# Turning the softmax maxima: on TensorE with a copy by ScalarE, or in 32 by 32 squares on VectorE with four DMAs

## The reference

```python
def _L0_xattn_ref(q, k, v, wq_w, wq_b, wk_w, wk_b, wv_w, wv_b, wo_w, wo_b):
    wq = (q @ wq_w.T + wq_b).reshape(b, t, H, DH)
    wk = (k @ wk_w.T + wk_b).reshape(b, t, H, DH)
    wv = (v @ wv_w.T + wv_b).reshape(b, t, H, DH)
    scores = jnp.einsum('bthd,bshd->bhts', wq, wk) / jnp.sqrt(jnp.float32(DH))
    probs = jax.nn.softmax(scores, axis=-1)
    attn = jnp.einsum('bhts,bshd->bthd', probs, wv)
    return attn.reshape(b, t, d) @ wo_w.T + wo_b

x = x + _L0_xattn_ref(_layernorm(x), ctx_1024, ctx_1024, ...)
x = x + _L0_ffn_ref(_layernorm(x), Wg, ln_scale, ln_bias, W1, b1, W2, b2)   # 8 experts, the best one by its logit
```

## Time and profile before

| | |
|---|---|
| median of 3 runs | 1424.43 us (1423.45 to 1425.28) |
| the profiled execution | 1425.39 us, of which the span from the first to the last instruction is 1423.6 us |
| mean granted TensorE clock | 0.992 |
| busy, share of the span | TensorE 97%, its weight loads 84%, VectorE 81%, ScalarE 69%, GpSimd 34% |
| 48 to 975 us (attention): busy | TensorE 907.6, VectorE 788.7, ScalarE 676.4, GpSimd 276.0 of 927 us |
| DMA | 168870 packets, 207.46 MB, 146 GB/s in the mean |

### The profile page before, as it was taken

The page is one execution under the profiler, slowest core; times in us unless marked ns, Lnnn a source line. Parts: engine busy times, 40 slices in busy tenths (PEclk is TensorE's granted clock), DMA queues, the critical chain, the costliest instruction groups (busy, mean ns, idle before and its releaser), DMA issues.

```text
span 1423.6 us, 40094 instructions
## 1 busy us (share of the span) xinstructions
PE 1380.6 (97%) x15314; PEld 1196.9 (84%) x15314; DVE 1158.0 (81%) x2760; ACT 985.6 (69%) x1664; POOL 482.8 (34%) x662
## 2 busy tenths in 40 slices
PE   6899999999999999999999999988999999999998
PEld 5688888888888888888888888876888888888887
DVE  4688888888888888888888888876787878878776
ACT  5477777777777777777777777756667666676764
POOL 4222332233322332233223332324444444444430
PEclk8899999999999999999999999999999999999999
DMA  6656665567656665667566755643343434434322
GB/s 183 144 146 184 171 185 150 159 172 178 161 150 175 174 176 151 167 174 182 154 159 168 185 152 154 167 114 105 91 126 106 127 105 120 117 108 132 102 80 75
DMA packets 168870, 207.46 MB, mean 146 GB/s; under 512 B 19895, under 2 KB 119530, under 8 KB 168682
## 3 DMA queue, kind: packets, MB, share of 16 engines
q1 hardware_dynamic: 168682, 204.89, 54.2%
HBM read 69.26 MB, written 33.81 MB: 72 GB/s over the span
## 4 chain that ended last, share of the span: by engine, by line
PE 88%; DVE 6%; ACT 2%; issue 2%; DMA 1%; POOL 0%; SPq 0%; ACTq 0%; DVEq 0%; POOLq 0%
PE s_ps L1345 13%; PE pp_ps L1219 11%; PE st_ps L1153 8%; PE pv_ps L1167 8%; PE s_ps L1125 8%; PE pp_ps L1192 7%; PE pp_ps L1227 6%; PE st_ps L1370 6%; PE pp_ps L1370 6%; PE pv_ps L1175 4%; PE pp_ps L1213 3%; DVE negmax L830 2%; PE pp_ps L1309 2%; PE t_ps L1144 2%; PE t_ps L1320 1%
## 5 line engine op out<-in xcount | busy, mean ns | idle before, releaser
L644 ACT ACTIVATE pT<-st_ps 128x1024 f32<-128x1024 f32 x256 | 263.1, 1028 | 108.0 <-PE st_ps L1153 107.1
L830 DVE TENSOR_REDUCE negmax<-s_ps 128x8 f32<-128x1024 f32 x256 | 311.2, 1215 | 24.3 <-PE s_ps L1125 24.0
L501 POOL TENSOR_TENSOR q_parts<-q,q_parts 128x1024 bf16<-128x1024 f32 x32 | 68.5, 2141 | 403.3 <-ACT q_parts L638 403.3
L700 ACT ACTIVATE pT<-s_ps,c 128x512 f32<-128x512 f32 x128 | 87.8, 688 | 119.4 <-PE s_ps L1345 114.3
L1125 PE MATMUL s_ps<-k_packed,q_packed 96*128 96x128 bf16 x2048 | 158.0, 220 | 11.2 <-DVE negmax L830 5.8
L1345 PE MATMUL s_ps<-k_packed,w_hi 128*128 128x512 f32 x512 | 165.8, 415 | 0.0
L1153 PE MATMUL st_ps<-q_packed,k_packed 98*128 98x128 bf16 x2048 | 158.1, 220 | 1.5 <-DMA q_packed<-negmaxT 1.5
L1125 PEld LDWEIGHTS s_ps<-k_packed,q_packed 96*128 96x128 bf16 x2048 | 128.1, 98 | 29.7 <-DVE negmax L830 17.5
L1153 PEld LDWEIGHTS st_ps<-q_packed,k_packed 98*128 98x128 bf16 x2048 | 120.6, 98 | 27.3 <-issue 25.0
L513 POOL TENSOR_TENSOR xb<-xin,bo_all 128x256 f32<-128x256 f32 x128 | 90.4, 728 | 150.8 <-DMA x_scratch<-xb 133.1
L1167 PE MATMUL pv_ps<-pT,v 128*32 128x128 f32 x4096 | 138.7, 276 | 0.0
(11 more groups left out here) (199 smaller groups left out, 3679.1 us busy)
## 6 DMA issues: line engine op xcount, KB each, us to landing
q_packed<-q_parts SPq DMA_DIRECT2D x192, 256.0 KB, 4.3
k_packed<-k_parts SPq DMA_DIRECT2D x192, 256.0 KB, 4.6
xin<-in_x_dram SPq DMA_DIRECT2D x32, 512.0 KB, 3.9
cin<-in_ctx_dram SPq DMA_DIRECT2D x32, 512.0 KB, 4.6
out_dram<-xb SPq DMA_DIRECT2D x32, 512.0 KB, 3.2
x_scratch<-xb SPq DMA_DIRECT2D x32, 256.0 KB, 4.8
x_scratch<-xb SPq DMA_DIRECT2D x64, 128.0 KB, 4.7
k_parts<-mask_scratch SPq DMA_DIRECT2D x32, 256.0 KB, 4.0
```

The source lines that it names most:

```text
L644: a.activation(pT[u % 2][:], st_ps[:], ACT.Exp, scale=DH ** -0.5).then_inc(s_exp, 1)
L700: a.activation(hidden32[m], h_ps[m % 2], ACT.Gelu, bias=c1[:, m:m + 1]).then_inc(f_he, 1)
L830: v.tensor_reduce(own, s_ps[:].rearrange("p (h s) -> p h s", s=P), AX_X, ALU.max, negate=True).then_inc(s_red, 1)
```

## The change

VectorE has an instruction that turns each square of 32 by 32 elements in place of the whole tile. `negmax_wide` becomes `negmax_hl`, 128 x 32, and after the low half of the second unit of a batch VectorE turns it into `negmaxT`, now 128 x 32: the strip of partitions 32q to 32q + 31 holds the 32 kinds (half, head) for the 32 queries 32q to 32q + 31. Four DMAs take the four strips to `q_packed`, each 32 rows of 64 bytes. They add 64 to the semaphore for a batch. `turn_max`, `keep_max`, the cleared columns and their semaphores are gone; `turn_attn` no longer waits for the copy of the maxima.

```diff
-        negmax_wide = [sb(f"negmax_wide{n}", [P, P], BF16) for n in range(2)]
-        negmaxT = [sb(f"negmaxT{n}", [2 * H, P], BF16) for n in range(2)]
+        negmax_hl = [sb(f"negmax_hl{n}", [P, 2 * H], BF16) for n in range(2)]
+        negmaxT = [sb(f"negmaxT{n}", [P, 2 * H], BF16) for n in range(2)]
...
             def load_max(n, b):
-                sp.wait_ge(s_mte, at(PAIRS, n, b + 1))
-                sp.dma_start(packed[0][n % 2][KP:KP + 2, :, b * T:(b + 1) * T], negmaxT[b % 2][:]).then_inc(ld_mx[b % 2], 16)
+                sp.wait_ge(s_mt, at(PAIRS, n, b + 1))
+                for q in range(P // (2 * H)):
+                    strip = slice(q * 2 * H, (q + 1) * 2 * H)
+                    sp.dma_start(packed[0][n % 2][KP:KP + 2, :, b * T + q * 2 * H:b * T + (q + 1) * 2 * H],
+                                 negmaxT[b % 2][strip, :]).then_inc(ld_mx[b % 2], 16)
...
-            def keep_max(n, b):
-
-                act.wait_ge(s_mt, at(PAIRS, n, b + 1))
-                wait(act, ld_mx[b % 2], 16 * at(PAIRS // 2, n, b // 2))
-                a.copy(negmaxT[b % 2][:], maxT_ps).then_inc(s_mte, 1)
...
                 v.tensor_tensor(lo, own, hi, ALU.subtract).then_inc(s_mp, 1)
+                if m == C - 1:
+                    dve.wait_ge(s_mp, at(UNITS, n, u + 1))
+                    wait(dve, ld_mx[b % 2], 64 * at(PAIRS // 2, n, b // 2))
+                    v.transpose(negmaxT[b % 2][:], negmax_hl[b % 2][:]).then_inc(s_mt, 1)
...
-            def turn_max(n, b):
-                pe.wait_ge(s_mp, at(UNITS, n, C * (b + 1)))
-
-                wait(pe, s_mte, at(PAIRS, n, b))
-                done = turned_at(n, C * b - 2) if b > 0 else turned_at(n - 1, UNITS - 2)
-                if done:
-                    pe.wait_ge(s_ate, at(GB, *done) + 1)
-                t.transpose(maxT_wide, negmax_wide[b % 2][:], ident_bf[:]).then_inc(s_mt, 1)
...
             def scoresT(n, u):
...
-                pe.wait_ge(ld_mx[b % 2], 16 * (at(PAIRS // 2, n, b // 2) + 1))
+                pe.wait_ge(ld_mx[b % 2], 64 * (at(PAIRS // 2, n, b // 2) + 1))
```

More of the change, by code:

```diff
@@ L128, in xattn_moe @@
         w1_raw = pT[1][:].rearrange("p (c e h) -> p c e h", c=C, e=E)
-        negmax_p = [wide[:, 0:2 * H].rearrange("p (i j m) -> p i j m", i=2, m=C) for wide in negmax_wide]
+        negmax_p = [hl[:].rearrange("p (i j m) -> p i j m", i=2, m=C) for hl in negmax_hl]
         recip = sb("recip", [P, H])
@@ L193, in xattn_moe @@
             "ffn_bias_in_psum", "ffn_bias_kept", "bo_in_psum", "ffn_weights_step"))
-        s_rowh, s_wide = sem("bias_rows_by_head"), sem("max_columns_cleared")
+        s_rowh = sem("bias_rows_by_head")
         ld_x, ld_c = [sem(f"x_loaded{n}") for n in range(2)], sem("ctx_loaded")
@@ L207, in xattn_moe @@
         s_r, s_mid, s_lo = sem("remainder_done"), sem("mid_done"), sem("lo_done")
-        s_s, s_red, s_hi, s_mp, s_mt, s_mte, s_st, s_exp, s_pv, s_rc, s_nrm = (sem(n) for n in (
-            "scores_ready", "max_done", "max_hi_done", "max_parts_done", "max_transposed", "max_kept",
+        s_s, s_red, s_hi, s_mp, s_mt, s_st, s_exp, s_pv, s_rc, s_nrm = (sem(n) for n in (
+            "scores_ready", "max_done", "max_hi_done", "max_parts_done", "max_transposed",
             "scoresT_ready", "exp_done", "pv_ready", "recip_done", "attn_normed"))
@@ L483, in _ @@
             g.memset(far_sel[:], 0.0).then_inc(s_pc, 1)
-            for wide in negmax_wide:
-                g.memset(wide[:, 2 * H:P], 0.0).then_inc(s_wide, 1)
             def norm(n):
@@ L678, in _ @@
                 item(1, k)
-            keep_max(0, 0)
             def keep_xT(n, c):
@@ L721, in group @@
                 for u in range(UNITS):
-                    nxt = later(n, u, 2)
                     done = turned_at(n, u)
@@ L741, in group @@
                             item(n + ahead, k)
-                    if nxt and u % 2 == 0:
-                        keep_max(nxt[0], nxt[1] // 2)
                     if more2 and u == 2:
@@ L1127, in scores, with turn_attn @@
                 mm.then_inc(s_s, 1)
-            def turn_max(n, b):
-                pe.wait_ge(s_mp, at(UNITS, n, C * (b + 1)))
-                wait(pe, s_mte, at(PAIRS, n, b))
-                done = turned_at(n, C * b - 2) if b > 0 else turned_at(n - 1, UNITS - 2)
-                if done:
-                    pe.wait_ge(s_ate, at(GB, *done) + 1)
-                t.transpose(maxT_wide, negmax_wide[b % 2][:], ident_bf[:]).then_inc(s_mt, 1)
-            def turn_attn(n, b, kept):
+            def turn_attn(n, b):
                 pe.wait_ge(s_nrm, at(GB, n, b + 1))
-                if kept:
-                    pe.wait_ge(s_mte, at(PAIRS, kept[0], kept[1] // 2 + 1))
+                if n == 0 and b == 0:
+                    pe.wait_ge(s_bo, 1)
+                wait(pe, s_ate, at(GB, n, b))
                 for c in range(C):
@@ L1292, in _ @@
             item(1, 5)
-            pe.wait_ge(s_wide, 2)
-            turn_max(0, 0)
             scores(0, 2)
@@ L1375, in even @@
             def even(n, u):
-                ahead, nxt, done, kept = later(n, u, 3), later(n, u, 2), turned_at(n, u), turned_at(n, u + 1)
+                ahead, done, kept = later(n, u, 3), turned_at(n, u), turned_at(n, u + 1)
                 if ahead:
@@ L1395, in odd @@
             def odd(n, u):
-                ahead, nxt, done = later(n, u, 3), later(n, u, 1), turned_at(n, u)
+                ahead, done = later(n, u, 3), turned_at(n, u)
                 if ahead:
@@ L1406, in odd @@
                 if done:
-                    turn_attn(*done, nxt)
+                    turn_attn(*done)
                 if n == LAST and u == 7:
@@ L1423, in _ @@
             hidden(0, 1)
-            turn_attn(LAST, GB - 1, None)
+            turn_attn(LAST, GB - 1)
             mask(0)
```

4 lines of the change are left out of this document (removed).

## The result

The changed kernel is slower: 1468.76 us in the median (1466.94 to 1470.10) against 1423.94 us before, a ratio of 1.0317 (95% interval 1.0303 to 1.0331). That is 44.8 us more. The forecast was 22 us more, so the sign was right, the size was half of what came, and 1468.8 lies above the range, which ended at 1466. The span of the profiled execution is 1466.9 us.

The account below looks back on a forecast made before the run. The prediction took TensorE, busy for 97% of the span, to bound the kernel. It summed -8 (TensorE) + 15.5 (VectorE) + 14 (packs) = +21.5 us to 1446 us, with a range of 1421 to 1466 us.

Parts of the forecast that it names:

- TensorE's 128 turns, -8 us: Attention stage on TensorE: 128 turns removed, each freeing a start-to-start slot of 0.065 us, 8 us saved.
- VectorE's turn, +15.5 us: 128 turns added on VectorE, each delaying it 0.24 us; TensorE loses 0.50 us a group in u=6, u=2 and u=0.
- SyncE's four DMAs, the shift: SyncE at batch 2: four DMAs take 2.75 us instead of one's 0.66, so the last k packs go 1.04 us later.
- How much of 1.04 us TensorE sees: First scores of the next group: DMA engines' backlog absorbs part of the packs' shift, leaving 0.45 us a group, 14 us.
- TensorE also comes 0.13 us earlier.: Before the next group's first scores: TensorE arrives 0.13 us sooner, two of its turns being gone, which lengthens its wait.
- Step u=4 was priced at 0: VectorE's turn in step u=4: aT_lo is ready 0.54 us before TensorE uses it, so the delay costs 0.
- nothing is absorbed: Rival, chance 0.1: the packs' shift reaches TensorE in full and two engines fall behind, 34 to 46 us, 1466 to 1478.
- two DMA engines that fall behind from 136 packets: Four DMAs of 64-byte rows are 136 packets on two engines, which may leave them 0.9 us behind at batch 1.
- The rule on the transposes: Trainium skill recommends VectorE for squares of 32; holding here would be the faster rival, 1417 us, chance 0.15.

Follow-up runs that it names:

- neither: The changed kernel without VectorE's turn and with one DMA of the maxima instead of four (some rows hold wrong values); 1412.5 us against 1422.6 before (0.9927).
- one_dma: The changed kernel with VectorE's turn but only the first of the four DMAs of the maxima; 1425.9 us, 1.0020 of the kernel before.
- no_vector_turn: The changed kernel without VectorE's turn, its four DMAs taking the strips of the maxima as they are (wrong values); 1454.2 us.
- gpsimd_later: The changed kernel with GpSimd's two residual additions after the store of x2 waiting one unit longer, until step u=4's halves of the maxima are done; 1473.0 us (1.0367).
- rows8_dma: The kernel before with its one DMA of the maxima cut into four by rows, each 8 rows of 256 bytes; 1539.5 us (1.0825).
- late_and_halved: The changed kernel with VectorE's turn behind aT_lo, u=6's halves behind cT's remainder, and ScalarE's queue issuing two of four DMAs per batch; 1439.5 us (1.0106).

## Why the prediction was right on the sign and wrong on the size

- **TensorE's 128 turns, -8 us.** Measured -10 us with ScalarE's copy (neither against before). The slot from start to start was the right reading: each of the four places is 0.07 to 0.1 us shorter, 0.30 us a group. But 0.19 of it comes back in the waits before the scores of u=0, u=2 and u=6, and 0.15 is the packs' wait, which is gone in neither because SyncE issues the packs 1.4 us earlier. That the sum lies so near to 8 is in part luck.
- **VectorE's turn, +15.5 us.** Measured +14.5 on the kernel before, 13.4 between neither and one_dma, 14.5 between no_vector_turn and the changed kernel. Its length (0.21 us), its delay (0.25 us) and the places u=6, u=0 and u=2 were right. The price in u=0 and u=2 was 0.16 to 0.17 instead of 0.13 us, and in u=6 0.18 instead of 0.24, as a stop costs TensorE 0.1 us beyond the wait (last section), and some comes back later.
- **SyncE's four DMAs, the shift.** The price (2.75 us for four; measured 2.65) and the shift of the last packs at batch 2 (1.04; measured 1.06) were right.
- **How much of 1.04 us TensorE sees: the step that failed.** It was put at 0.45 us a group, 14 us, because one straggling engine in the tail of the earlier trace rows was read as a backlog that would absorb the rest. Measured: 42 to 43 us for the three added DMAs. By the table the moment of the scores moved by 0.99 for 1.06 us, and extra_at_packs, which delays SyncE there by one DMA and does nothing else, passes 0.52 of 0.65 us on. A straggler that ends 0.25 us before the scores says that there is no slack. It says nothing about the backlog at the place where the four DMAs stand, 5 us earlier. There the engines do have one, and it ends before the last packs come: the share falls to 0.28 for a microsecond, and all that is behind it lands later by the whole shift.
- **Why 43 and not 31 x 1.06 = 33 us.** The count starts from one_dma, not from before. With one DMA and no trip over TensorE and ScalarE, SyncE issues the packs at 6.44 instead of 7.63 us, and the scores don't wait. Three more DMAs put the packs 2.25 us later. About half of that is spare there, and the scores start 1.12 us later (11.21 to 12.33), 31 x 1.12 = 35 us. The four stretches at 1.2 GHz add 6.5 us, a cost that no term of the prediction had.
- **"TensorE also comes 0.13 us earlier."** It came 0.34 us later (11.19 to 11.53), which the packs' wait covered. Step u=4 was priced at 0 and aT_lo cost 0.23 us there; that was wrong as a reading and without effect on the time, as gpsimd_later shows.
- **The rival "nothing is absorbed" (1466 to 1478 us, chance 0.1) is what happened,** by its first half. Its second, two DMA engines that fall behind from 136 packets, is not supported: rows8_dma with half of the packets costs more. Its argument, that the shift is sure if its price is, deserved more than the 0.1, and the range should have held it.
- **The rule on the transposes** (the Trainium skill, "VectorE: DVE Perf Modes", "Rules for kernel authors") calls VectorE's transpose the fastest for squares of 32. Of the two durations that is so here: the 0.21 us of the turn are less than TensorE's 0.23 us; but TensorE's slot was 0.06 to 0.08 us and VectorE's is on TensorE's path, so this kernel lost 3 us by that exchange before the DMAs are counted.

## What to carry to other kernels

Count the DMAs that a queue issues between the event that releases them and the one that somebody waits for: each cost 0.6 to 0.7 us there in these runs, with 8 KB as with 2 KB, and a small transfer in four parts can cost more than all the instructions that it saves. Treat a delay ahead of a landing without slack as passed on in full, unless an experiment with one idle DMA at that place shows otherwise, and look at the DMA share between the two: a backlog helps only as long as it lasts until the next issue. A stop also costs beyond its length when the granted clock falls behind it. Of two waits that end in the same place, removing the earlier one gives nothing.

## What else the runs showed

**A DMA's issue costs nearly the same for very different shapes.** The median is 0.60 us for a 256 KB pack, 655 ns for 32 rows of 256 bytes, and 655, 652, 604 and 602 ns for the four DMAs of 32 rows of 64 bytes in their order, so the place in the list counts as much as the shape. A single one can take longer: in the changed kernel one in ten of the k packs takes SyncE over 1.1 us.

**TensorE's stop costs more than its wait.** In u=0, u=2 and u=4 turn_pv starts 0.235 us after the last third of the output product where that has not waited (neither, late_and_halved) and 0.34 us after it where it has: 0.1 us for each stop.

**GpSimd and VectorE.** The high half took 0.69 us instead of 0.17 at 528.35. GpSimd's timeline beside it:

```profile
527.60 1.42 POOL L512 TENSOR_TENSOR xb<-xin,bo_all 128x256 f32<-128x256 f32 x2 [3.08 <-DMA x_scratch<-xb]
```

GpSimd ends at 529.02 and VectorE's operation at 529.04. One of the two halves is stretched like this, to over 0.3 us, 39 times after the change and 19 times before, always while GpSimd runs, and mostly until 0.02 to 0.03 us after GpSimd's end. GpSimd waits longer for the store in the changed kernel (181.3 us in all instead of 133.1), which would move it onto VectorE's operation; in neither and one_dma no half is stretched at all. The Trainium skill, "SBUF — State Buffer", section "SBUF: two separate sides", says that a VectorE operation with two inputs in SBUF and a GpSimd operation that reads SBUF share a pair of ports that one of them holds for its whole instruction; both halves have two such inputs, and the trace agrees.
